# Idle products from the first microsecond, and ahead of the first projection and scores

## The reference

```python
...
Q = (h @ Wq.T).reshape(b, n, H, d).transpose(0, 2, 1, 3)
K = (h @ Wk.T).reshape(b, n, H, d).transpose(0, 2, 1, 3)
sim = jnp.einsum('bhnd,bhmd->bnm', Q, K) / (jnp.sqrt(jnp.float32(d)) * H)
k = max(1, int(n * TOP_K_RATIO))            # 153 of 512
threshold = jax.lax.top_k(sim, k)[0][:, :, -1:]
A = jax.nn.sigmoid(sim) * (sim >= threshold)
A = (A + jnp.swapaxes(A, -1, -2)) * 0.5
x = x + tanh(g_xattn) * ((1 - gamma) * layernorm(x) + gamma * A)
...
# experts on layernorm(x): softmax gate, the best 2 of 8, fc1 -> gelu -> fc2, 512 wide
x = x + tanh(g_ffn) * sum over the two experts of weight * alpha * expert(layernorm(x))
```

## Time and profile before

| What | us |
|---|---|
| median of 3 runs | 364.29 (364.28 to 367.03) |
| span of the profiled execution | 363.4 |
| its own time | not listed apart from the span; the median is 0.89 above the span |
| busy in it: PE, DVE, ACT, POOL | 324.3 (89%), 200.7 (55%), 165.0 (45%), 100.1 (28%) |

### The profile page before, as it was taken

One profiled execution on the slowest core, in us unless ns is written; L12 is line 12 of the kernel. 1 busy time (PEld: TensorE's weight loads), 2 busy tenths in 40 slices (PEclk: granted clock), 3 DMA queues, 4 the chain that ended last, 5 costly groups with the idle time before them and its releaser, 6 DMA issues.

```text
span 363.4 us, 6131 instructions
## 1 busy us (share of the span) xinstructions
PE 324.3 (89%) x1937; PEld 232.9 (64%) x1937; DVE 200.7 (55%) x697; ACT 165.0 (45%) x384; POOL 100.1 (28%) x141
## 2 busy tenths in 40 slices
PE   6906899779998999899999989999999999999960
PEld 4402667677764786678778576777785877577610
DVE  0488698887879777898886372636206112311010
ACT  2485515389996746256786222232222213132320
POOL 5001001361111357114307431331733111312031
PEclk9975699899999999999999999999999999999996
DMA  2999989977974696876627587744678854533253
GB/s 91 379 392 369 352 298 331 378 267 139 305 145 123 144 243 231 146 161 183 113 54 181 191 173 135 211 100 81 203 163 149 176 119 104 111 64 87 30 74 46
DMA packets 53636, 65.79 MB, mean 181 GB/s; under 512 B 9792, under 2 KB 28512, under 8 KB 53600
## 3 DMA queue, kind: packets, MB, share of 16 engines
q1 hardware_dynamic: 46144, 47.99, 43.7%
q0 software_dynamic: 7456, 17.37, 24.7%
HBM read 39.56 MB, written 25.78 MB: 180 GB/s over the span
## 4 chain that ended last, share of the span: by engine, by line
PE 50%; issue 18%; DVE 14%; DVEq 5%; DMA 5%; POOL 3%; POOLq 2%; ACT 2%; ACTq 0%
PE ps L1711 21%; PE ps L1684 13%; PE ps L1694 10%; DMA out_rows<-ab,dst 3%; PE ps L1647 2%; POOL xs_rows L566 2%; DMA meta<-xs_rows 2%; DVE top L1087 1%; DVE stats L1012 1%; PE ps L1607 1%; PE ps L1721 1%; PE ps L1627 1%; PE ps L1639 1%; POOLq L530 1%; DVEq L1086 1%
## 5 line engine op out<-in xcount | busy, mean ns | idle before, releaser
L1684 PEld LDWEIGHTS ps<-xgT_r,weights 128*128 128x128 f32 x768 | 87.8, 192 | 8.3 <-issue 6.7
L1684 PE MATMUL ps<-xgT_r,weights 128*128 128x128 f32 x768 | 89.6, 276 | 3.6 <-ACT xgT_r L743 2.0
L1711 PE MATMUL ps<-weights,act_r 128*128 128x512 f32 x192 | 86.3, 595 | 1.5 <-ACT act_r L766 1.5
L580 POOL DMA_INDIRECT out_rows<-ys,dst x24 | 37.9, 1578 | 115.2 <-ACT ys L773 70.0
L1711 PEld LDWEIGHTS ps<-weights,act_r 128*128 128x128 f32 x192 | 34.9, 190 | 38.4 <-issue 36.5
L766 ACT ACTIVATE act_r<-ps,b1T 128x128 f32<-128x128 f32 x96 | 27.1, 365 | 38.9 <-PE ps L1684 38.8
L1694 PEld LDWEIGHTS ps<-sim,weights 128*128 128x128 f32 x256 | 35.2, 190 | 1.9 <-issue 1.7
L566 POOL DMA_INDIRECT xs_rows<-ab,pos x32 | 31.9, 998 | 14.5 <-issue 9.1
L1694 PE MATMUL ps<-sim,weights 128*128 128x160 f32 x256 | 35.6, 299 | 0.0
L773 ACT ACTIVATE ys<-ys,meta 128x512 f32<-128x512 f32 x24 | 17.3, 719 | 31.3 <-DVE ys L1322 31.3
L1322 DVE TENSOR_TENSOR ys<-ps,b_r 128x512 f32<-128x512 f32 x24 | 16.5, 686 | 23.4 <-PE ps L1711 22.0
(11 more groups left out here) (206 smaller groups left out, 419.0 us busy)
## 6 DMA issues: line engine op xcount, KB each, us to landing
weights<-in_L_ffn_fc_w SPq DMA_DIRECT2D x16, 1024.0 KB, 8.0
b_r<-in_L_ffn_fc_b SPq DMA_DIRECT2D x32, 256.0 KB, 4.1
xg_r<-xs_rows SPq DMA_DIRECT2D x88, 64.0 KB
xb<-in_x SPq DMA_DIRECT2D x4, 1024.0 KB, 7.1
out_rows<-xb SPq DMA_DIRECT2D x4, 1024.0 KB, 5.5
sim<-xs_rows SPq DMA_DIRECT2D x32, 80.0 KB
xs_rows<-weights SPq DMA_DIRECT2D x1, 2064.0 KB, 13.5
xs_rows<-weights SPq DMA_DIRECT2D x2, 516.0 KB, 5.9
```

What stands on the lines that cost most here:

```text
L580: pool.indirect_dma_start(out=out_rows, out_offset=bass.IndirectOffsetOnAxis(ap=dst[:, k % 2, e:e + 1], axis=0), in_=result_rows(m), in_of ...
L1684: mm = pe.matmul(ps[:, n % 2, i * P:(i + 1) * P], weights[:, e, 0, h, i * P:(i + 1) * P], rows[:, h * P:(h + 1) * P], start=(h == 0), stop ...
L1711: mm = pe.matmul(ps[:, 2 + m % 2, :], rows, weights[:, e, 1, i, :], start=(i == 0), stop=(i == IB - 1))
```

## The change

The memset of ones_b goes to the head of GpSimd's list and signals a semaphore of its own, fill_ok. TensorE waits for that and runs 16 idle products (BUSY_FIRST), then waits for the identity as before and runs the 24. Eight more idle products stand behind the wait for m_qk, ahead of the projection of batch 0, and eight ahead of its scores. No other line changes.

```diff
-BUSY_LOADS, BUSY_SEARCH, BUSY_MASK = 24, 36, 48
+BUSY_FIRST, BUSY_LOADS, BUSY_SEARCH, BUSY_MASK = 16, 24, 36, 48
...
-        over_ok = sem("over_ok")
+        over_ok, fill_ok = sem("over_ok"), sem("fill_ok")
...
         @block.gpsimd
         def _(pool):
+            pool.memset(ones_b[:], 1.0).then_inc(fill_ok, 1)
             pool.memset(zeros, 0.0).then_inc(consts, 1)
             pool.memset(ident[:], 0.0)
-            pool.memset(ones_b[:], 1.0)
             pool.memset(ones_col[:], 1.0)
             pool.memset(ones, 1.0)
...
+            pe.wait_ge(fill_ok, 1)
+            keep_busy(BUSY_FIRST)
             pe.wait_ge(consts, 2)
             keep_busy(BUSY_LOADS)
             pe.wait_ge(qk_in, 32)
             pe.matmul(ps[:, 0, 0:C], wq, wk, start=True, stop=True).then_inc(m_ps, 1)
             turn_context(0)
             pe.wait_ge(m_sb, 1)
+            keep_busy(8)
             project(0)
+            keep_busy(8)
             for t in range(BT):
                 scores(0, t)
```

## The result

The changed kernel takes 364.14 us (median of 17 runs, 361.84 to 364.74), the kernel before, run beside it, 365.53 (17 runs, 363.91 to 367.11): ratio 0.9957, 95% interval 0.9938 to 0.9977. It is faster by 0.4%, and the forecast of 361.2 us was wrong: the time lies just above the range. Two later series of 12 runs gave 0.9995 [0.9961, 1.0029] and 0.9961 [0.9935, 0.9987]. (The comparisons leave disturbed runs out.) The sign came out as forecast, and that the change stays within 1%; of the 3.05 us forecast 1.39 were measured.

A forecast was written before the change was run, and what follows sets the result against it. Before 113 us the threshold-search chain on VectorE and ScalarE, waiting for batch 0's scores, sets the time. Gains 2.85 + 0.2 = 3.05 us take the span from 363.4 to 360.35; with 0.89 around it, 361.2 us, range 359.9 to 364.0.

The forecast's parts named there:

- The coefficients as the wait that comes last: ScalarE, ahead of the projection's copy: coefficients wait for scalar loads, so it starts at 9.13 instead of 9.47, 0.34 us gained.
- Eight fills before the projection: TensorE, under ScalarE's copy of the transposes: cost 0 if the clock is fast, 0.1 us if slow.
- before the scores: 0: TensorE, eight fills under the projection's copy: 0.52 us fast, cost 0; slow they would cost 0.2 us.
- The rise: TensorE's clock going from 1.2 to 2.4 GHz: at 6.3 us, 5.2 us after the first fill, instead of about 15.4.
- 36 fills at 37 us: TensorE ahead of the sum VectorE waits 0.70 us for: a sooner clock rise gains up to 0.7, taken as 0.2.
- Then the chain runs as before, 2.85 us earlier: After the scores' last statistic, 14.2 us instead of 17.05: order unchanged, everything follows 2.85 us earlier.
- From 113 us to 351 us ... can be shortened only by an earlier start: TensorE's late part, busy 234.37 of 238 us: only starting it earlier shortens it.
- gained and given back: Rival: the second clock rise, at 42.6 us, fails until 49, 2.4 us lost, or loads come no earlier; 364.0 us, chance 0.10.
- an early start that is gone by 113 us: Sign that would show the gained-and-given-back rival: the lead won at the start lost before 113 us.
- that stays: Time around the profiled span: the runs' median, 364.29, lies 0.89 us above it, assumed the same after the change.
- The first rival: Late rise: transposes break the stretch, clock rises at about 12.2 us, gain 1.15, 363.1 us; chance 0.11.
- The slower rival: TensorE, 5.02 to 16.4 us: no rise before the scores are done, fills only stand in the way; 365.0 us, chance 0.04.

The follow-up runs named there:

- e6: Changed kernel with ScalarE's copy of the projection moved ahead of the coefficients; 362.88 us, ratio to before 0.9935.
- e1: Changed kernel without its two loops of eight idle products; 364.67 us, ratio to before 0.9974.
- e2: Changed kernel without its first sixteen idle products, the eights kept; 363.09 us, ratio to before 0.9953.
- r14: Changed kernel run again unchanged, as reference in a later series; 363.92 us, ratio to before 0.9961.
- l11: Kernel before, unchanged, profiled once more; 365.11 us, span 363.4.
- l12: Kernel before, unchanged, profiled yet once more; 365.51 us, span 363.7.
- e4: Kernel before with 28 idle products between the picking of rows and layer 1; 364.58 us, ratio to before 0.9982.
- e9: e7 plus 24 idle products ahead of the first picking of rows and 40 ahead of layer 1; 362.45 us, ratio to before 0.9926.
- e7: e6 plus VectorE taking the first two score tiles' statistics ahead of x's; 363.71 us, ratio to before 0.9959.
- e16: Kernel before, start untouched, with 24 idle products ahead of the first picking of rows and 40 ahead of layer 1; 365.36 us, ratio to before 0.9975.
- e15: Changed kernel without its sixteen, with 24 idle products ahead of the first picking of rows and 40 ahead of layer 1; 363.94 us, ratio to before 0.9953.

## Why the prediction was wrong, point by point

**The first 17 us: right but for the rise.** First fill 1.12 (1.11 worked out), the copy of the projection at 9.05 (9.13), copies of the scores from 10.83 to 13.57 (10.93 to 13.6), last statistic 14.20 (14.2). The coefficients as the wait that comes last: shown by e6, in which the copy no longer stands behind them and the statistics move. "Eight fills before the projection" and "before the scores: 0", because they lie under a copy: right as a cost, but I gave them no use beyond that; the one trace without them, e1, has 1.6 us less (−1.27 against −2.85), by a fall of the clock at the scores. The sixteen were given the rise; e2 shows it without them. The rise was put at 6.3 us, 5.2 at the earliest. It came at 4.8 us in the trace of after and between 3.9 and 7.1 in the nine others that begin with the sixteen: the delay that I took from two rises and one stretch is no constant. That the start came out to 0.01 us all the same is due to the coefficients, which capped it.

**36 fills at 37 us, taken at 0.2:** the wait of VectorE fell from 0.70 us to 0.21, so 0.5. From trace to trace it differs: with the second rise at 38 us r14 wins 0.8, with that at 41 us e2 loses 0.3. Timeline of VectorE, after:

```profile
39.87 0.14 DVE L1109 CAST proved_i<-ps 1x1 int32<-1x1 f32 x1 [0.21 <-PE ps L1614]
```

**"Then the chain runs as before, 2.85 us earlier": right up to the seam, and by two errors that cancel.** TensorE comes to the seam 2.77 us earlier. The fills at 37 us gave 0.5 instead of 0.2, and a term that I did not have took 0.6: the clock fell behind the wait at 75 us, and of the 1.63 us lost there 1.05 came back by the seam, where TensorE's wait went from 0.98 to 0.43 us. Five traces with that wait idle and five with it filled show this cause. It is not the earlier chain that made the wait long: it is 3.5 us where the picking of rows ran at full clock, at any lead. Timeline of TensorE, after:

```profile
110.30 1.23 PE L1627 MATMUL ps<-ident,ab 128*128 128x128 f32 x8 [0.43 <-DVE xb L1149]
```

**"From 113 us to 351 us ... can be shortened only by an earlier start": the step that failed.** I took this part as a fixed length, so that each microsecond won ahead of it would reach the end. It is not fixed. From the seam to the last product the first trace of before takes 238.95 us, the other traces with the late rise 239.1 to 239.9, and the three of the changed kernel 240.3, 240.4 and 242.1. So the lead of 2.77 us at the seam is 1.43 at the end, and in r14 3.04 us are nothing. As far as the traces show, the length is made by waits for rows (at 152 and 213 us) and, in r14, by the fall at 119 us, 3.3 us by itself; no run moved or removed either. I had read one trace, and it was the shortest.

How much of this the change itself brings stays open. Some of the 1.34 us lost by after is the luck of the trace that it is set against: l11, l12 and e4 lose 0.6 to 0.95 us there with no earlier start. The early traces without such a fall take 0.7 us more on average than the five with the late rise (240.2 against 239.5), but the two groups overlap, and e9, with the largest lead, takes 239.5. A wait for rows does not grow with the lead either, as l11 and e7 show.

My rival of "gained and given back" was this in kind. It sought the place at the second rise (42 to 49 us), which came early enough in every trace, and held that no wait for a DMA stood against the rest. Its sign, "an early start that is gone by 113 us", did not come. (A slip besides: by its own sum the low end of the range is 360.5 less 0.5, so 360.0 and not 359.9.)

The runs of the changed kernel agree that falls of the clock have a part. Of its 17, eight with a mean granted clock of 0.955 to 0.957 take 361.84 to 363.17 us, nine with 0.942 to 0.954 take 364.14 to 364.74. Its median is the lowest of the second group. In the two later series the order is looser (364.12 us at 0.958, 363.25 at 0.954), so it is a tendency and no law.

**The base.** "The median is 364.29, 0.89 above" the span, "that stays": the profiled execution of after has 1.8 us around its span, a second trace of before as well (363.4 and 365.11), so the first trace of before stood for about 365.2 us, and the runs of before beside these kernels have medians of 364.8 to 365.6. With 1.8 in place of 0.89 the forecast would have been 362.15, of which the trace itself (362.98) misses 0.8 and the median 2. This is a mis-sized term, not a mechanism. Of the 2.9 us between forecast and result, 1.2 are the base (364.29 against 365.53) and 1.7 are gain that did not come.

**The rise.** I took one trace of before as what the kernel always does. e16 shows that its start can rise at 7.0 us without the change. How often it does can't be read from times, since a fall later on moves them as much; if it were one run in five, the change would win 2.3 us at the start on average and not 2.9. That share stays open. The first rival, that transposes break a stretch of work, falls: in the seven traces with the sixteen or the eights in which the rise comes during or right after the transposes (6.0 to 7.1 us), and in e16, it does not wait for the 12.2 that this rival needs. The five that rise before or at the first transpose (3.9 to 5.2 us) say nothing of it. The Trainium skill, "TensorE: Matmul & The Clock Gate", Part 1, says that the number of slow products at the start differs from run to run of one kernel; the rises at 7.0 and at 14.9 to 15.3 us behind the same start agree. The slower rival fell too: no trace with the early fills had slow scores but e1, which lacks the eights.

What stays open: why the rows come late at 152 and 213 us in some executions (the transfers ahead of them were not moved in any run), and what brings the falls at 55, 119 and 214 us in some and not in others.

## What to carry to other kernels

When idle products win time at the start, follow the lead event by event to the end before you bank it. A drop of the lead half way, like the 1.6 us at 76 us here, is not yet a loss: at the next place where TensorE waits for the chain, two thirds of it were back. A part of the kernel in which TensorE is 98% busy has no fixed length either; take it from several traces, since its spread (239.0 to 239.9 us in the five traces with the late rise) was a third of the gain at stake. Fill long waits together with the change if a trace shows a fall behind them, and judge by medians of a dozen runs, for one trace with the early rise (or without) says little of how often it comes.

## What was not expected of the hardware

The clock fell to 0.50 with TensorE busy throughout: 6.6 of 6.6 us in r14 from 119.7 us, behind 128x8 products and transposes; e6 and e15 have the same stretch, and it took 3.3 us of r14's lead. The low stretch at 76 us cost TensorE 1.6 us and the kernel 0.6 at the seam; in the kernel before, a stretch of the same length at 66.5 us lies in work with 2.0 us of waiting behind it. And the unchanged start raised the clock either 4.5 us after its first fill (e16) or 12.4 to 12.9 us after it (the other four traces of it), with the same instructions up to there.
